# A copy of the first product goes ahead of the rounding of the block two further on: the order of one scalar queue in a two-convolution stage

## The reference

```python
def _L3_conv_ref(x, w1, w2, gamma1, beta1, mean1, var1, gamma2, beta2, mean2, var2):
    ...
    residual = x
    out = _conv3x3(x, w1, stride=1)
    out = jax.nn.relu(_bn(out, gamma1, beta1, mean1, var1))
    out = _conv3x3(out, w2, stride=1)
    out = _bn(out, gamma2, beta2, mean2, var2)
    return jax.nn.relu(out + residual)
...
x = x + _L3_conv_ref(_gn(x), L3_conv_w1, L3_conv_w2, ...)
```

## Time and profile before

| | us |
|---|---|
| median of 3 runs | 4019.54 (4017.68 to 4019.99) |
| profiled execution, own time | 4019.97 |
| its span | 4018.2 |
| last stage, from its first L917 | from 3524.4 on |
| PE busy | 3715.9 (92%) |
| DVE busy | 2301.8 (57%) |
| ACT busy | 2135.5 (53%) |
| POOL busy | 1671.3 (42%) |

### The profile page before, as it was taken

The page is one execution under the profiler, slowest core; times in us unless marked ns, Lnnn a source line. Parts: engine busy times, 40 slices in busy tenths (PEclk is TensorE's granted clock), DMA queues, the critical chain, the costliest instruction groups (busy, mean ns, idle before and its releaser), DMA issues. The chain is left out here.

```text
span 4018.2 us, 108193 instructions
## 1 busy us (share of the span) xinstructions
PE 3715.9 (92%) x31044; PEld 3178.0 (79%) x31044; DVE 2301.8 (57%) x5980; ACT 2135.5 (53%) x5953; POOL 1671.3 (42%) x2962
## 2 busy tenths in 40 slices
PE   7989898989899998969999999999999799978888
PEld 4656566666666665669999999999999688878887
DVE  6868686877778786843333333333333322277777
ACT  5868686877778787844443333333333322045544
POOL 3746373746556464710013333333344311055554
PEclk9999999999999999989999999999999899989999
DMA  4111111111111111111100000000022000000000
GB/s 165 40 55 39 55 40 55 40 54 40 50 44 37 57 40 56 40 64 52 47 37 0 0 0 0 0 0 0 0 63 61 22 0 0 12 17 17 33 33 33
DMA packets 170031, 140.29 MB, mean 35 GB/s; under 512 B 31776, under 2 KB 158368, under 8 KB 166688
## 3 DMA queue, kind: packets, MB, share of 16 engines
q1 hardware_dynamic: 138400, 123.78, 9.4%
q10 hardware_dynamic: 31360, 12.87, 1.2%
HBM read 83.32 MB, written 53.22 MB: 34 GB/s over the span
## 5 line engine op out<-in xcount | busy, mean ns | idle before, releaser
L193 PE MATMUL bank<-h,w_hh 128*128 128x128 f32 x8032 | 933.8, 275 | 0.0
L193 PEld LDWEIGHTS bank<-h,w_hh 128*128 128x128 f32 x8032 | 917.1, 192 | 0.0
L1448 ACT ACTIVATE Pr<-bank,nmx 128x256 f32<-128x256 f32 x1568 | 722.6, 473 | 276.6 <-DVE nmx L1551 270.8
L238 ACT ACTIVATE h<-bank,bg 128x128 f32<-128x128 f32 x1008 | 370.7, 368 | 818.0 <-PE bank L193 817.9
L1385 POOL TENSOR_TENSOR Pr<-Pr,rden 128x512 f32<-128x512 f32 (+1 forms) x784 | 659.6, 855 | 165.9 <-DVE rden L1611 135.8
L1551 DVE TENSOR_REDUCE nmx<-bank 128x1 f32<-128x256 f32 x1568 | 555.1, 417 | 155.6 <-PE bank L1711 154.4
L1375 POOL COPY kg<-kT 128x64 f32 x1568 | 300.2, 238 | 597.2 <-DMA row<-ix 295.2
L284 DVE SCALAR_TENSOR_TENSOR inp<-bank,b_in,tz 128x256 f32<-128x256 f32 x196 | 85.8, 480 | 697.4 <-ACT tz L221 697.4
L1457 ACT ACTIVATE PT<-bank 128x512 f32<-128x512 f32 x784 | 428.8, 610 | 21.4 <-PE bank L1724 21.3
L1724 PE MATMUL bank<-ident,Pr 128*128 128x128 f32 x3136 | 437.5, 283 | 0.0
L1724 PEld LDWEIGHTS bank<-ident,Pr 128*128 128x128 f32 x3136 | 342.7, 143 | 81.1 <-issue 71.7
(11 more groups left out here) (248 smaller groups left out, 7098.0 us busy)
## 6 DMA issues: line engine op xcount, KB each, us to landing
vg<-v_windows SPq DMA_DIRECT2D x1176, 32.0 KB, 2.0
first_gates<-gate_sums SPq DMA_DIRECT2D x28, 512.0 KB, 2.6
gate_sums<-first_gates SPq DMA_DIRECT2D x28, 512.0 KB, 3.6
X<-in_x SPq DMA_DIRECT2D x8, 1568.0 KB, 17.6
vg<-v_windows ACTq DMA_DIRECT2D x392, 32.0 KB, 2.3
x_backup<-X SPq DMA_DIRECT2D x8, 1568.0 KB, 5.9
out<-X SPq DMA_DIRECT2D x7, 1568.0 KB, 5.1
v_windows<-vst SPq DMA_DIRECT2D x56, 192.0 KB, 2.1
```

The lines of the kernel that those rows point to most:

```text
L193: ins = pe.matmul(bank[m][:, tt * COLS:(tt + 1) * COLS], w_hh[:, k, m * 128:(m + 1) * 128], prev[:, k, :], start=False, stop=(k == NH - 1) ...
L238: act.activation(h[:, 2 * q + tt, m, :], bank[m][:, tt * COLS:(tt + 1) * COLS], ACT.Tanh, bias=bg[:, 0, m:m + 1]).then_inc(s_h, 1)
L1448: act.activation(Pr[:, par, j, :], bank[j][:, 0:KEYS], ACT.Exp, bias=nmx[:, par, j:j + 1], accum_out=den[:, par, j:j + 1])\
```

## The change

On the scalar engine, `first(q)` is called before `hi(q + 2)` and no longer after it.

```diff
                     if q:
                         finish(q - 1)
+                    first(q)
                     if q + 2 < NQ:
                         hi(q + 2)
-                    first(q)
                     if 3 <= r < 3 + NRB and n + 1 < B:
                         z_block(n + 1, r - 3)
```

## The result

The changed kernel takes 3998.19 us (median of 5 runs, 3997.03 to 3999.1), the kernel before 4019.54 us beside it; the ratio is 0.9948 with a 95% interval of 0.9933 to 0.9962. That is 21.4 us less, where 19.5 were forecast. The span went from 4018.2 to 3996.4 us.

The account below looks back on a forecast made before the run. Turns at SBUF between L887 and vector instructions with two SBUF tensors were taken to bound the last stage; 13.9 (middle blocks) + 5.8 (adding blocks) = 19.7 us off 4019.97 gave 4000 us, range 3995 to 4009.

Parts of the forecast that it names:

- step 4: 29 adding blocks: L1013 goes between GpSimd's two L887 halves; 0.2 us gained each, 5.8 us in all.
- Step 1: Copy L923 is done about 0.65 us into the block; L997's 1.44 us wait for it goes to zero.
- step 2: The two L917, now behind the copy, still wait for points at 1.25 us: cost nothing, cover 0.6 us.
- Step 3: 24 middle blocks: L984 still waits for L887, so 6.95 becomes 6.37 us; 0.58 each, 13.9 us.
- Rival A: GpSimd keeps its turn through both L887 halves, so only the middle blocks gain: 4006 us, chance 0.26.
- C: Gain given back through stretching, or hand-overs of 0.3 to 0.6 us in adding blocks: 4012 to 4020, chance 0.08.
- B: Turns do not bind: adding blocks lose the whole wait, middle blocks fall to TensorE's 6.5 us; 3967 us, chance 0.03.
- D: Vector engine keeps the turn through L1016, delaying GpSimd's second half: 4018 (chance 0.02) or 4029 (0.03).
- Step 5: TensorE needs 6.5 us a block; the second half's 0.8 us delay is less than its 1.58 us waiting: cost nothing.
- The check on TensorE's waits: In the profile after, TensorE's waits for L887 should be less by the whole gain.

Follow-up runs that it names:

- the chained waits: Changed kernel with one, then three 128x1 memsets ahead of each L1013, each waited for by semaphore: stage 478.6 and 479.4 us, against 470.7.
- the run with only this part: Kernel before, with the copy moved ahead only in iterations in front of middle blocks: 4003.43 us against 4018.18, ratio 0.996.
- the run with this part alone: Kernel before, with the copy moved ahead only in iterations in front of adding blocks: 4010.11 us, ratio 0.9981.

## Why the prediction was right

**What bounds.** That vector instructions with two SBUF tensors and L887 take turns was the step that carried the forecast. The runs bear it out: the 89 us of waiting that went brought 22, the chained waits show a turn lost and not a delay added, and with L887 gone the stretching is gone. Two readings were looser than they sounded. The rule names two SBUF tensors, but L805, which the sum leans on in step 4, has one and was held as well. And the earlier trace rows shows L997 to L1007 only with GpSimd busy; the last two blocks of that trace, with GpSimd idle, give the same 0.56 to 0.57 us.

**Step 1** (the copy is early, the wait goes to zero) and **step 2** (L917 not delayed): right; 1.3 us of waiting is left, and L917 starts 1.24 us after L984. Where L908 runs, the scalar engine had 0.2 us to spare behind it, where 0.15 was worked out.

**Step 3**, 24 x 0.58 = 13.9 us: 6.95 became 6.37, and the run with only this part gave a stage 14.6 us shorter. What the prediction didn't foresee is the L984 of 2.47 us in the block between, held through a whole half; it cost nothing, because that block's length stayed.

**Step 4**, 29 x 0.2 = 5.8 us: the mechanism was right, the size a little small. The block came out at 7.97, the lower of the two values worked out (7.97 to 8.07); the 0.1 us that I had added for handing over is not there. The stage was 7.8 us shorter in the run with this part alone. The two parts, 14.6 and 7.8, are 2.7 us more than the 19.7 of the sum; the stage itself gained 22.1, the medians 21.4, so the forecast of 19.5 was about 2 us short, most of it in this step.

**Rival A** (GpSimd keeps both halves) lost by less than 0.15 us: L1013 comes at 4.23, and it would be locked out from somewhere between 4.31 and 4.37 us. The prediction had given its own margin as 0.1 us, so that the forecast and not A came true was in part luck. Its price was right, too: locked out, the block is 8.24 us. **C** is out: the blocks show no cost of the hand-over. **B** is out as a description of this kernel, but TensorE's limit, which it set at 6.5 us a block, is what is found once L887 is out of the way, at 6.40. **D** didn't occur: of the 32 L1016, 29 lost to GpSimd's second half, 0.03 us behind L1013.

**Step 5**, TensorE: cost nothing, right, but for a reason that I had stated too weakly: its limit holds over an image. **The check on TensorE's waits**: I wrote that its waits for L887 fall by the whole gain. They fell from 71.5 to 54.6 us, 17 of 22; the waits of its weight loads, which the profile counts apart, fell from 69.3 to 47.6, the whole 22.

## What to carry to other kernels

A wait that a profile charges to an engine is worth its length only if nothing else was in use beside it. Here GpSimd's subtraction ran under the wait, the next vector instruction needed the same turn at SBUF, and 1.43 us of wait were worth 0.58 and 0.27 us. To find such a turn, look for one instruction with two durations, and check whether its stretched end keeps a fixed distance to another engine's end; then add up the turns in a block, and shorten the longest by giving its work to the engine that does it faster (1.13 us against 2.13 for this half), which brought another 46 us here where the reordering had brought 22.

## What the runs showed of the hardware

A turn is lost all at once. An addition that starts at 4.23 to 4.31 us goes first and takes its 1.03 us; one that comes from a semaphore wait and starts at 4.37 to 4.46 us waits 1.8 us or more for GpSimd's second half, and at 4.63 us still 1.6. This kernel's gain in adding blocks, 8 us, hangs on 0.1 us.

The end of a held instruction keeps its distance from GpSimd's recorded end: 0.83 us for all 29 L1013 before and all 29 L1016 after, which is 0.20 and 0.15 us less than they last alone, and 0.48 us for every held L984, 10 before and 34 after, 0.14 us less.

In the run with the 128x448 memset the addition behind it started at 4.7 us and still went first, and behind the 128x128 one at 4.38 us, while with a semaphore wait in between it was locked out at the same 4.38 us. Whether the memset held the turn for it or the addition had asked while it was queued is open; no run separates them, and the one late block of the two runs fits neither.

The stage in the slowest version (the half moved, the old order) was granted a lower TensorE clock, 0.93 to 0.95 in windows of 100 us between 3600 and 4000 us, where the changed kernel and the kernel before had 1.00 in the window of 3700 to 3800. Whether that made the stage longer isn't shown: an image took 62.5 us where 62 were expected, and eight times that difference, 4 us, is about what it came out above its expectation (3 to 7 us).
